# Linear attention with a routed expert layer: the token turn moves from TensorE to VectorE's block transposes, and the batch loop is written in another order

## The reference

```python
xn = layernorm(x)
q, k, v = heads(xn, Wq, bq), heads(xn, Wk, bk), heads(xn, Wv, bv)     # 16 heads of 8
qp = relu(einsum('bhsd,hdf->bhsf', q, rw)) + EPS                      # 64 features a head
kp = relu(einsum('bhsd,hdf->bhsf', k, rw)) + EPS
kv = einsum('bhsf,bhsd->bhfd', kp, v)
out = einsum('bhsf,bhfd->bhsd', qp, kv) / (einsum('bhsf,bhf->bhs', qp, kp.sum(2)) + EPS)
attn = out @ Wo + bo
# each row goes to the one of 8 experts with the largest logit xn @ wr + br
gate = top_p[:, 0] / (top_p[:, 0] + top_p[:, 1])
ffn = gate * (gelu(xn @ w1[e] + b1[e]) @ w2[e] + b2[e])
x + attn + ffn
```

## Time and profile before

| | |
|---|---|
| runs | 217.41, 218.32, 218.95 us; median 218.32 us |
| profiled execution | 218.47 us, of which the traced span is 216.4 us |
| TensorE busy | 201.2 us, 93% of the span |
| VectorE busy | 131.1 us, 61% |
| ScalarE busy | 124.1 us, 57% |
| GpSimd busy | 140.7 us, 65% |

### The profile page before, as it was taken

The page is one execution under the profiler, slowest core; times in us unless marked ns, Lnnn a source line. Parts: engine busy times, 40 slices in busy tenths (PEclk is TensorE's granted clock), DMA queues, the critical chain, the costliest instruction groups (busy, mean ns, idle before and its releaser), DMA issues. The chain is left out here.

```text
span 216.4 us, 6736 instructions
## 1 busy us (share of the span) xinstructions
PE 201.2 (93%) x2291; PEld 162.8 (75%) x2291; DVE 131.1 (61%) x422; ACT 124.1 (57%) x293; POOL 140.7 (65%) x163
## 2 busy tenths in 40 slices
PE   6789996989999999999999999999999999999960
PEld 6466764556676676767766767999999999999960
DVE  5877744779777666677777673554544445544440
ACT  3366988345546655556556585656665555666520
POOL 2498941232188877878778510078888888888885
PEclk9999999699999999999999999999999999999996
DMA  4929999990012111112114882199999999999141
GB/s 134 272 48 266 213 116 255 299 233 6 3 49 64 64 61 55 46 52 64 64 50 114 270 231 70 48 232 199 178 207 215 204 215 199 194 213 198 10 36 10
DMA packets 32192, 29.53 MB, mean 136 GB/s; under 512 B 5505, under 2 KB 24481, under 8 KB 32161
## 3 DMA queue, kind: packets, MB, share of 16 engines
q1 hardware_dynamic: 25520, 24.88, 46.1%
q0 software_dynamic: 6640, 4.24, 12.3%
HBM read 20.17 MB, written 11.49 MB: 146 GB/s over the span
## 5 line engine op out<-in xcount | busy, mean ns | idle before, releaser
L412 POOL DMA_INDIRECT out<-k_all,slots_all x39 | 61.1, 1567 | 23.6 <-issue 23.3
L738 ACT ACTIVATE q_all<-feat,w_slot 128x128 f32<-128x128 f32 x156 | 44.5, 368 | 28.3 <-PE feat L591 20.8
L591 PE MATMUL feat<-v_all,w_slot 128*128 128x128 f32 x312 | 41.2, 275 | 0.0
L380 POOL DMA_INDIRECT sorted_x<-rows_all,place_i x32 | 31.9, 995 | 13.0 <-PE feat L477 8.0
L591 PEld LDWEIGHTS feat<-v_all,w_slot 128*128 128x128 f32 x312 | 38.0, 192 | 0.0
L695 ACT ACTIVATE k_feat<-feat 128x1024 f32<-128x1024 f32 x16 | 16.4, 1024 | 19.8 <-PE feat L477 19.8
L702 ACT ACTIVATE q_feat<-feat 128x1024 f32<-128x1024 f32 x16 | 16.4, 1027 | 15.5 <-PE feat L488 15.5
L884 DVE TENSOR_SCALAR q_feat<-feat 128x1024 f32<-128x1024 f32 x16 | 19.6, 1225 | 8.8 <-PE feat L488 8.8
L488 PE MATMUL feat<-q_all,rw_bd 32*128 32x256 f32 x256 | 18.8, 408 | 3.8 <-DVE k_feat L877 1.9
L337 POOL TENSOR_SCALAR rows_all<-x_all,meanvar,rstd 128x128 f32<-128x128 f32 x21 | 16.8, 811 | 7.8 <-DVE rstd L770 7.7
L601 PE MATMUL o_bank<-w_sb,q_all 128*128 x160 | 21.2, 275 | 0.0
(11 more groups left out here) (120 smaller groups left out, 314.5 us busy)
## 6 DMA issues: line engine op xcount, KB each, us to landing
w_slot<-w1x SPq DMA_DIRECT2D x39, 258.0 KB
sorted_x<-ones_f SPq DMA_DIRECT2D x1, 2535.0 KB, 20.2
x_all<-in_x SPq DMA_DIRECT2D x8, 256.0 KB, 4.1
w1x<-in_w SPq DMA_DIRECT2D x1, 2048.0 KB, 25.6
out<-res SPq DMA_DIRECT2D x16, 128.0 KB
slots_all<-sorted_x SPq DMA_DIRECT2D x23, 65.0 KB
out<-k_all,slots_all POOLq DMA_INDIRECT x39
slots_all<-sorted_x SPq DMA_DIRECT2D x1, 520.0 KB, 5.1
```

Source lines behind the costliest of these rows:

```text
L380: pool.indirect_dma_start(sorted_x, bass.IndirectOffsetOnAxis(ap=place_i[:, t:t + 1], axis=0), rows_all[:, t, :], None).then_inc(x_moved, 16)
L412: pool.indirect_dma_start(out_rows, bass.IndirectOffsetOnAxis(ap=slot_rows[j % SLOT_RING][:, D + 1:XW].bitcast(I32), axis=0), y_sb[j % Y_R ...
L591: ins = pe.matmul(bank[:, a * P:(a + 1) * P], w1_slot[j % W1_RING][:, a * P:(a + 1) * P], xsT[j % X_RING][:, :], start=True, stop=True)
L738: act.activation(hidden_T[j % H_RING][:, a * P:(a + 1) * P], hid_bank[j % HID][:, a * P:(a + 1) * P], ACT.Gelu, bias=w1_slot[j % W1_RING][ ...
```

## The change

The four transposes of a batch's outputs and the two that turn them back leave TensorE. VectorE transposes blocks of 32 by 32 instead: `turn_tokens` turns `pk` (128x512) into `pk_tok` and takes the reciprocal; `scale_tokens` multiplies and turns 128x256 back into `attn_T`. `pk` is laid out in blocks for this, and `ka` holds only the key-value sums.

`q_relu` evicts three of the four query banks on ScalarE and one on VectorE. In the loop TensorE runs `turn` ahead of `q_features`, and `out_project` behind `q_features` and for one batch later (i-3 in place of i-4). On VectorE `residual(i-4)` now stands behind `q_relu(i)` and `scale_tokens(i-2)`. The output bias is added to x in the first four iterations. Of three moves of rows in an iteration, one follows the key features and two the query features, where it was two and one. The last batches stand ahead of the first slots, and batch 15 gets a bank of its own. In chunks 1 and 2 GpSimd normalises two tiles in place of three.

```diff
+TB = 2 * HD
...
-KF_MOVES = {i: 2 for i in range(FIRST_MOVES, 15)}
-QF_MOVES = {i: 1 for i in range(FIRST_MOVES, 14)}
+KF_MOVES = {i: 1 for i in range(FIRST_MOVES, 14)} | {14: 2}
+QF_MOVES = {i: 2 for i in range(FIRST_MOVES, 14)}
...
-NORM = [0] + [3] * (CHUNKS - 1)
+NORM = [0, 2, 2] + [3] * (CHUNKS - 3)
...
-        ka = [sb(f"ka{n}", [P, 2 * S], F32) for n in range(2)]
-        pk = [sb(f"pk{n}", [P, 2, S], F32) for n in range(2)]
-        inv_den = sb("inv_den", [P, K * H], F32)
-        attn_tok = [sb(f"attn_tok{n}", [P, K, D], F32) for n in range(2)]
+        ka = [sb(f"ka{n}", [P, S], F32) for n in range(2)]
+        pk = [sb(f"pk{n}", [P, S // TB, 2, TB], F32) for n in range(2)]
+        pk_tok = sb("pk_tok", [P, 2 * S // TB, TB], F32)
+        inv_den = sb("inv_den", [P, 2 * S // TB, 2], F32)
+        attn_tok = sb("attn_tok", [P, S], F32)
+        attn_T = [sb(f"attn_T{n}", [P, S], F32) for n in range(2)]
...
+        last_bank = feat[0][:, 512:1024]
...
-                if i >= 1:
-                    out_bias(i - 1)
                 if i + 1 < NBATCH:
                     spread_v(i + 1)
                 pool.wait_ge(qf_ps, i + 1)
                 moves(QF_MOVES.get(i, 0))
-                add_out_bias(i)
+                if i >= 1:
+                    out_bias(i - 1)
+                if i < FIRST_MOVES:
+                    for b in range(NBATCH // FIRST_MOVES * i, NBATCH // FIRST_MOVES * (i + 1)):
+                        add_out_bias(b)
             out_bias(NBATCH - 1)
...
             def turn(i):
                 due(pe, ka_ready, i - 1)
-                if i <= NBATCH:
-                    pe.wait_ge(kv_ready, 2 * i)
-                    for par in range(2):
-                        ins = pe.transpose(kt_bank[:, par * P:(par + 1) * P], kv_T[(i - 1) % 2][:, par, :], ident[:, :])
-                if i >= 3:
-                    pe.wait_ge(tok_ready, i - 2)
-                    for k in range(K):
-                        ins = pe.transpose(kt_bank[:, S + k * P:S + (k + 1) * P], attn_tok[(i - 3) % 2][:, k, :], ident[:, :])
+                pe.wait_ge(kv_ready, 2 * i)
+                for par in range(2):
+                    ins = pe.transpose(kt_bank[:, par * P:(par + 1) * P], kv_T[(i - 1) % 2][:, par, :], ident[:, :])
                 ins.then_inc(turn_ps, 1)
...
-                due(pe, tok_ready, b)
+                if b < NBATCH - 1:
+                    due(pe, pk_ready, 2 * b)
+                bank = o_bank if b < NBATCH - 1 else last_bank
...
-            def turn_outputs(b):
-                pe.wait_ge(pk_ready, 2 * (b + 1))
-                for k in range(K):
-                    for par in range(2):
-                        ins = pe.transpose(strided(o_bank[:, k * S + par * GD:k * S + par * GD + 1], [(2 * GD, G), (1, GD)]),
-                                           pk[b % 2][:, par, k * P:(k + 1) * P], ident[:, :])
-                ins.then_inc(pkT_ps, 1)
-
             def out_project(b):
-                pe.wait_ge(ka_ready, b + 3)
+                pe.wait_ge(tok_ready, b + 1)
                 due(pe, r_ready, b)
                 for k in range(K):
-                    ins = pe.matmul(wo_bank[:, k * D:(k + 1) * D], ka[(b + 3) % 2][:, S + k * P:S + (k + 1) * P], wo_sb[:, :],
+                    ins = pe.matmul(wo_bank[:, k * D:(k + 1) * D], attn_T[b % 2][:, k * P:(k + 1) * P], wo_sb[:, :],
                                     start=True, stop=True)
                 ins.then_inc(wo_ps, 1)
...
                 if i >= 2:
                     outputs(i - 2)
-                if i == 4:
-                    pe.wait_ge(placed, 2)
-                    pe.wait_ge(wo_in, 16)
-                if i >= 4:
-                    out_project(i - 4)
-                q_features(i)
-                if i >= 2:
-                    turn_outputs(i - 2)
                 if i >= 1:
                     turn(i)
+                q_features(i)
+                if i == 3:
+                    pe.wait_ge(placed, 1)
+                    pe.wait_ge(wo_in, 16)
+                if i >= 3:
+                    out_project(i - 3)
                 key_values(i)
...
+            outputs(14)
+            turn(16)
+            out_project(13)
             turn_slot(0)
-            outputs(14)
-            pe.wait_ge(kv_ready, 2 * NBATCH)
+            outputs(15)
             turn_slot(1)
-            turn(16)
-            out_project(12)
-            turn_outputs(14)
-            out_project(13)
-            outputs(15)
-            turn(17)
             up(0)
-            turn_outputs(15)
+            out_project(14)
             turn_slot(2)
+            pe.wait_ge(pk_ready, 2 * NBATCH)
             up(1)
-            out_project(14)
-            turn(18)
+            out_project(15)
             turn_slot(3)
             up(2)
             read_expert(0)
...
-                act.activation(q_feat[s][:, 0:NC // 2, :].rearrange("p c n -> p (c n)"), feat[0][:, :], ACT.Relu) \
+                act.activation(q_feat[s][:, 0:NC // 2, :].rearrange("p c n -> p (c n)"), feat[0][:, :], ACT.Relu)
+                act.activation(q_feat[s][:, NC // 2:3 * NC // 4, :].rearrange("p c n -> p (c n)"), feat[1][:, 0:512], ACT.Relu) \
                     .then_inc(q_act, 1)
...
-                due(act, pkT_ps, b - 1)
+                due(act, pk_turned, b - 1)
+                bank = o_bank if b < NBATCH - 1 else last_bank
                 for par in range(2):
-                    act.activation(pk[s][:, par, :], o_bank[:, par * S:(par + 1) * S], ACT.Identity,
+                    act.activation(pk[s][:, :, par, :], bank[:, par * S:(par + 1) * S].rearrange("p (t r) -> p t r", r=TB), ACT.Identity,
                                    bias=o_bias[s][:, par:par + 1]).then_inc(pk_ready, 1)
...
-                due(act, wo_ps, i - 4)
-                act.activation(ka[i % 2][:, lo:hi], kt_bank[:, lo:hi], ACT.Copy).then_inc(ka_ready, 1)
+                act.activation(ka[i % 2][:, :], kt_bank[:, 0:S], ACT.Copy).then_inc(ka_ready, 1)
...
-                q_relu(i)
                 if i >= 1:
                     save_turned(i)
+                q_relu(i)
...
-                dve.tensor_scalar(q_feat[s][:, NC // 2:NC, :].rearrange("p c n -> p (c n)"), feat[1][:, :],
+                dve.tensor_scalar(q_feat[s][:, 3 * NC // 4:NC, :].rearrange("p c n -> p (c n)"), feat[1][:, 512:1024],
                                   0.0, None, ALU.max).then_inc(q_dve, 1)
...
-            def token_rows(b):
-                s = b % 2
-                dve.wait_ge(pkT_ps, b + 1)
-                dve.reciprocal(inv_den[:, :].rearrange("p (c h) -> p c h", h=2),
-                               strided(o_bank[:, HD:HD + 1], [(2 * HD, K * NC), (DK, 2)])).then_inc(inv_ready, 1)
+            def turn_tokens(b):
+                dve.wait_ge(pk_ready, 2 * (b + 1))
+                dve.transpose(pk_tok[:, :, :].rearrange("p n r -> p (n r)"),
+                              pk[b % 2][:, :, :, :].rearrange("p t a r -> p (t a r)")).then_inc(pk_turned, 1)
+                dve.wait_ge(pk_turned, b + 1)
+                dve.reciprocal(inv_den[:, :, :], strided(pk_tok[:, 0, HD:HD + 1], [(TB, 2 * S // TB), (DK, 2)])).then_inc(inv_ready, 1)
+
+            def scale_tokens(b):
                 dve.wait_ge(inv_ready, b + 1)
-                due(dve, turn_ps, b + 1)
-                dve.tensor_tensor(strided(attn_tok[s][:, 0, 0:1], [(HD, K * NC), (DK, 2), (1, DK)]),
-                                  strided(o_bank[:, 0:1], [(2 * HD, K * NC), (DK, 2), (1, DK)]),
-                                  strided(inv_den[:, 0:1], [(2, K * NC), (1, 2), (0, DK)]), ALU.mult).then_inc(tok_ready, 1)
+                dve.tensor_tensor(strided(attn_tok[:, 0:1], [(HD, 2 * S // TB), (DK, 2), (1, DK)]),
+                                  strided(pk_tok[:, 0, 0:1], [(TB, 2 * S // TB), (DK, 2), (1, DK)]),
+                                  strided(inv_den[:, 0, 0:1], [(2, 2 * S // TB), (1, 2), (0, DK)]), ALU.mult).then_inc(tok_scaled, 1)
+                dve.wait_ge(tok_scaled, b + 1)
+                due(dve, wo_ps, b - 1)
+                dve.transpose(attn_T[b % 2][:, :], attn_tok[:, :]).then_inc(tok_ready, 1)
 
             def mask_kv(b):
...
                 k_relu(i)
+                if i >= 2:
+                    turn_tokens(i - 2)
                 if i == 0:
                     pick(CHUNKS // 2 - 1)
+                q_relu(i)
+                if i == 0:
                     scan_rows()
+                    list_earlier()
+                if i >= 2:
+                    scale_tokens(i - 2)
+                if i >= 4:
+                    residual(i - 4)
+                mask_kv(i)
...
+            residual(12)
+            residual(13)
             save_xsT(0)
+            turn_tokens(14)
+            scale_tokens(14)
             save_xsT(1)
-            residual(12)
-            token_rows(14)
-            residual(13)
-            token_rows(15)
+            turn_tokens(15)
+            scale_tokens(15)
```

(10 more changed lines are left out.)

23 lines of the change are left out of this document (6 added, 17 removed).

## The result

The change takes 253.04 us (median, 252.53 to 253.47) against 218.63 (217.41 to 219.07) for the kernel before on the same chip: a ratio of 1.158, 95% interval 1.155 to 1.162. I forecast 260, between 242 and 270.

What follows compares the result with a forecast made beforehand. The prediction took TensorE's own list, 5.87 us an iteration, to bound the kernel before. Its sum was 218.5 + 23.8 + 5.0 + 14.4 - 1.1 - 0.8 = 259.8, stated as 260 us, range 242 to 270.

Steps and rivals of the forecast that it cites:

- The mechanism, its place and its sign: TensorE's projection waits for VectorE's residual, now last in the same iteration's list; slower, chance 0.96.
- The chain, +23.8: Loop through TensorE, ScalarE and VectorE, closed by projection waiting on residual: 7.85 us against 5.87, twelve iterations, 23.8 us.
- rival 2: VectorE's block transposes are dear, with rows as for the reduction: 7.9 us more, 268 us; chance 0.08.
- The clock, +14.4: TensorE's clock falls to half rate after each iteration's idle stretch: 1.2 us in each of twelve iterations, 14.4 us.
- rival 1: The projection stalls but TensorE's clock stays up: 245.4 us, or 240.4 if outputs aren't late either; chance 0.32.
- Outputs late beside a move, +5.0: Outputs reach ScalarE 0.55 us late beside a GpSimd row move, now uncovered: nine iterations, 5.0 us.
- At nothing: the output bias in four iterations: Twelve output-bias additions moved into GpSimd's idle time in the first four iterations: put at no cost.
- At nothing: the moved row moves: Two GpSimd row moves placed behind the query features: put at no cost, GpSimd being busy 48.29 of 60 us.
- At nothing: ScalarE's third bank and the tail: ScalarE's third query bank, with over 2 us free there, and the last batches' new order: both put at no cost.
- The end, -1.1: At the last scatters, residuals end earlier relative to the slots, so up to 1.1 us come back.
- The start, -0.8: GpSimd normalises one tile less in chunks 1 and 2, where TensorE waited: 0.8 us saved, between 0 and 1.6.

Runs made afterwards that it cites:

- the filled stall: The changed kernel with 18 unused identity transposes on TensorE between query features and projection from iteration 4 on: 241.68 us, ratio 1.108 to the kernel before.
- the fastest kernel: The changed kernel with residual(i-4) behind k_relu(i), x's output bias added once an iteration, and out_bias(i-1) ahead of v's spread: 211.56 us, ratio 0.971.

## Why the prediction was right, and where its steps failed

The mechanism, its place and its sign were right. That the sum came as near as it did is in part luck, since terms with errors of either sign met in it. Term by term (sum forecast 259.8, measured 253.04):

- **The chain, +23.8.** Right in kind, a little too large: 7.62 us an iteration, not 7.85. 18.7 us lie in eleven iterations of the loop and 1.6 in the end, where the projection of batch 13 and those behind it wait: from the key features of iteration 15 to the first matmul of slot 3 it is 18.9 us (155.36 to 174.30) for 16.6 (122.70 to 139.31). Of these 2.3 us, 0.7 are the half clock from 153 on, which reaches into this stretch (the kernel with the filled stall needs 18.2, 145.53 to 163.74). That makes 18.7 and 1.6, or 20.3. The estimates of the block transposes were 0.69 and 0.42, measured 0.71 and 0.45; rival 2 is out. I had summed whole durations on VectorE, but its next instruction starts up to 0.1 us before the recorded end of the one before (107.89, 108.63, 108.90, 109.45, 109.89, 110.26). The two links that are most off are the query bank, 0.55 for 0.69 (it lasts 0.63), and the reciprocal, 0.27 for 0.35. The wait was opened in two ways, and both times it went.
- **The clock, +14.4.** Too large: 11 by the filled stall, 10.3 by the profiles (9.6 in the loop, 0.7 behind it). I had given the fall to each of twelve iterations, and from iteration 4 on it came six times. Of rival 1 this much is true that an idle stretch of 2.3 us doesn't lower the clock each time. One fall costs a little more than I had allowed: 10.3 us over six falls is 1.7, where I said 1.2, at most 1.5. Too many falls and too small a price for each cancel in part.
- **Outputs late beside a move, +5.0.** Failed. In the change outputs reach ScalarE after 1.13 us with a move running (106.26 for 1.02), and so in seven of the ten iterations with one move; in the three others the clock is at half. Only iteration 14, which has two moves there, is late at full clock (1.69). Two moves behind the key features bring 0.5 us back, on the query features. Why a result is late beside some moves and on time beside others, I can't say from these traces: in the fastest kernel moves run beside outputs that arrive after 1.14 and query features that arrive after 1.20.
- **At nothing: the output bias in four iterations.** Failed. I looked only at whether GpSimd had the time, and not at what its additions do to VectorE's instructions beside them. It costs 3.6 us in the change and 1.4 once the residual is early.
- **At nothing: the moved row moves.** Right for this kernel (no wait on GpSimd's bias is in it, the bias starts at 111.17, the mask at 112.56) and a trap for every repair: with the projection put back, `out_bias` behind the two moves costs about 8 us (1.041 against 1.003).
- **At nothing: ScalarE's third bank and the tail.** The bank pays, by 3 us, though it does end up in the chain that bounds the fastest kernel. The tail's cost is counted with the chain.
- **The end, -1.1.** Failed: from the first matmul of slot 3 to the last scatter it is 73.75 us (174.30 to 248.05) for 73.49 (139.31 to 212.80). The first scatter follows slot 3 by 0.6 us less, and the last one loses that again: the end goes by when the slots start.
- **The start, -0.8.** 0.26 in the profile, 0.5 in the run of its own.

The terms that were too large (outputs 5.0, chain 3.5, clock 3.4) and those that were missing (bias 3.6, the end 1.4, the start 0.4) leave 6.5 us of the 6.8 by which the sum is too high.

The Trainium skill, VectorE: DVE Perf Modes, Rules for kernel authors, would have kept the 128x128 transposes on TensorE. I had it worth 13 us as long as the chain is closed. Once the residual is early, the kernel with transposes on VectorE is 2 to 3% faster than before, which speaks against the rule for this kernel. No run puts the transposes back on TensorE with everything else left in place, so that the gain comes from them and not from the other edits that remain is argued, not shown.

## What to carry to other kernels

When work moves from a full engine to one with room, look for a single buffer that both touch, and write down in which iteration each side's wait was satisfied before and now: one instruction's place was worth 38 us here, where the whole change, with the residual and GpSimd's bias well placed, gains 6. When one closed chain is opened, look for the next shorter one in the code, since the profile may show it only as idle time without a named releaser. An engine that is busy all the time can still be paced by such a chain: add up the chain's links before taking work off the engine. An engine's spare time is not a free place for work until the instructions that run beside it on other engines have been compared with and without that work.

## What the runs showed of the hardware

- Short VectorE instructions between SBUF tiles (128x8) took 0.65 to 0.67 us beside GpSimd's addition of 128x256 (0.70) and 0.17 without.
- VectorE's 32x32 block transposes of float32: 0.71 us for 128x512, 0.45 for 128x256.
- The granted clock was 1.00 through eleven iterations in which 2.2 us each were filled with transposes of the identity, and fell in six of them without.
- Results of TensorE came 0.5 to 0.6 us late beside some row moves of GpSimd (query features 1.74 against 1.20 us from their start, outputs 1.69 against 1.14) and on time beside others, with a cause that stays open.
